# Attention in a decoder layer: the scaling of a pair of tiles and its scatter one slot further behind the scores

## What is computed

```python
x = x + attention(layernorm(x), ...)                 # 8 heads, low-rank q and kv
x = x + experts1(layernorm(x), ctx, ...)              # 8 experts of width 512, the best 2 by ctx @ Wg + bg
x = x + experts2(layernorm(x), ...)                   # 32 experts of width 64, the best 8, and a shared one

# attention, for each sequence:
scores = einsum('bhsd,bhtd->bhst', q, k) * scale
attn = softmax(scores)
o = einsum('bhst,bhtd->bhsd', attn, v_c)
return o.reshape(b, s, H * DK) @ W_O + b_O
```

## Time and profile before

| | us |
|---|---|
| median of three runs | 674.77 |
| lowest and highest of them | 673.5 and 676.57 |
| the profiled execution, its own time | 676.88 |
| the span that its trace covers | 674.8 |
| of the span: from its start to PE's first product of F1 | 197.6 |

### The profile page before, as it was taken

One profiled execution on the slowest core, in us unless ns is written; L12 is line 12 of the kernel. 1 busy time (PEld: TensorE's weight loads), 2 busy tenths in 40 slices (PEclk: granted clock), 3 DMA queues, 4 the chain that ended last, 5 costly groups with the idle time before them and its releaser, 6 DMA issues.

```text
span 674.8 us, 11558 instructions
## 1 busy us (share of the span) xinstructions
PE 620.7 (92%) x3354; PEld 464.3 (69%) x3354; DVE 543.1 (80%) x1361; ACT 421.0 (62%) x775; POOL 344.9 (51%) x410
## 2 busy tenths in 40 slices
PE   8987888887859999999889989999999999999997
PEld 7655566555647888787767656777777767677873
DVE  4687799999976666876764787899999999989973
ACT  3684678774449998888776444664737566473530
POOL 6134858888775567874674663553808255000000
PEclk9987779998889999999899999999999999999999
DMA  8998013102434555544316734544536354444551
GB/s 216 308 384 250 17 52 102 33 32 60 124 95 129 173 169 167 182 156 157 94 68 156 157 82 110 151 119 123 147 96 174 94 149 121 127 113 124 146 158 31
DMA packets 77836, 90.20 MB, mean 134 GB/s; under 512 B 15361, under 2 KB 44011, under 8 KB 77774
## 3 DMA queue, kind: packets, MB, share of 16 engines
q1 hardware_dynamic: 72648, 80.96, 42.2%
q0 software_dynamic: 4288, 8.40, 4.3%
q10 hardware_dynamic: 838, 0.11, 0.1%
HBM read 64.48 MB, written 24.90 MB: 132 GB/s over the span
## 4 chain that ended last, share of the span: by engine, by line
PE 66%; DVE 10%; issue 5%; POOL 4%; ACT 3%; DVEq 0%; ACTq 0%
PE bank L1635 10%; PE bank L1637 10%; PE bank L1636 10%; PE pair_banks L1917 7%; PE pair_banks L1537 5%; PE score_banks L1635 4%; PE score_banks L1637 4%; PE score_banks L1636 4%; POOL x_sorted L606 3%; PE pair_banks L1635 2%; PE pair_banks L1637 2%; PE pair_banks L1636 2%; PE pair_banks L1722 1%; PE bank L1537 1%; POOL sm L590 1%
## 5 line engine op out<-in xcount | busy, mean ns | idle before, releaser
L967 ACT ACTIVATE r_s<-bank 128x512 f32<-128x512 f32 x136 | 80.7, 595 | 68.0 <-PE bank L1637 66.1
L1442 DVE TENSOR_TENSOR t_s<-rc_s,bcb 128x512 f32<-128x512 f32 x128 | 89.4, 701 | 4.8 <-PE pair_banks L1917 4.8
L606 POOL DMA_INDIRECT x_sorted<-xsb,posi x64 | 63.9, 998 | 28.5 <-issue 15.1
L681 POOL DMA_INDIRECT yg<-y_sorted,posi x64 | 68.9, 1077 | 17.6 <-issue 16.9
L1429 DVE TENSOR_TENSOR rc_s<-r_s,score_banks 128x512 f32<-128x512 f32 x90 | 61.2, 680 | 18.7 <-ACT r_s L967 15.3
L1635 PE MATMUL bank<-fxh,Gh 128*128 128x512 f32 x136 | 73.3, 539 | 0.0
L733 ACT ACTIVATE t_h<-t_s 128x512 fp32r<-128x512 f32 x72 | 45.3, 629 | 41.6 <-DVE t_s L1442 27.0
L1917 PE MATMUL pair_banks<-t_s,Dn 128*128 128x512 f32 x128 | 63.2, 591 | 0.0
L1502 DVE TENSOR_TENSOR t_l<-t_s,t_h 128x512 fp32r<-128x512 f32 x72 | 53.7, 746 | 0.2
L1637 PE MATMUL bank<-fxh,Gl 128*128 128x512 f32 x136 | 53.7, 395 | 0.0
L1636 PE MATMUL bank<-fxl,Gh 128*128 128x512 f32 x136 | 53.4, 393 | 0.0
(11 more groups left out here) (327 smaller groups left out, 1822.8 us busy)
## 6 DMA issues: line engine op xcount, KB each, us to landing
bcb<-c_rows SPq DMA_DIRECT2D x128, 256.0 KB, 4.0
wraw<-in_L_xattn_W SPq DMA_DIRECT2D x46, 256.0 KB, 2.9
x_sorted<-wraw SPq DMA_DIRECT2D x1, 5888.0 KB, 18.6
y_sorted<-wraw SPq DMA_DIRECT2D x1, 5888.0 KB, 33.7
xg<-x_sorted SPq DMA_DIRECT2D x23, 256.0 KB, 2.6
y_sorted<-ysb SPq DMA_DIRECT2D x23, 256.0 KB, 2.0
ctxb<-in_ctx SPq DMA_DIRECT2D x8, 256.0 KB, 5.7
out<-x_all SPq DMA_DIRECT2D x8, 256.0 KB
```

What stands on the lines that cost most here:

```text
L606: pool.indirect_dma_start(out=xs, out_offset=bass.IndirectOffsetOnAxis(ap=posi[:, m, c:c + 1], axis=0), in_=xsb[:, m % SC, :], in_offset=N ...
L681: pool.indirect_dma_start(out=yg[:, j % 2, t, c, :], out_offset=None, in_=ys, in_offset=bass.IndirectOffsetOnAxis(ap=posi[:, j * TPS + t, ...
L967: act.activation(r_s[:, n % RB2, :], bank[n % 3][:, :], ACT.Silu).then_inc(F["act"], 1)
L1442: tt(t_s[:, n % TB2, :], rc_s[:, n % CB2, :], bcb[:, p - 1, :], ALU.mult).then_inc(F["t"], 1)
```

## The change

The scaling (`xs`) and the scatter each get a lag one higher, and the loops of all engines run one slot more.

```diff
-LAG = dict(exp=1, sum=2, norm=3, pT=4, u=5, out=6, rstd=7, xs=8, scatter=9)
+LAG = dict(exp=1, sum=2, norm=3, pT=4, u=5, out=6, rstd=7, xs=9, scatter=10)
-TAIL = 10
+TAIL = 11
```

## The result

| | before | changed |
|---|---|---|
| median, same chip, four runs each | 675.17 | 681.95 |
| lowest and highest | 673.5, 676.57 | 680.68, 682.6 |
| ratio, 95% interval | | 1.0103 [1.0081, 1.0125] |
| the profiled execution, its own time | 676.88 | 681.92 |
| its span | 674.8 | 680.1 |

The change makes the kernel 1.0% slower, about 6.8 us. The forecast was 677.2 with a range to 681.5, so it was wrong. What came looks like the rival "more eps are held, slower" (682.1), though not under the condition that the prediction gave for it.

The account below looks back on a forecast made before the run. Attention has no single busiest engine; DVE's xsb and POOL's S4 alternate on the path. Slots 9 to 14 lose about 0.7, eight pairs take 67.6 after 66.9, `xl` starts 2.4 later: 677.2 against the 674.77 median, range 671.3 to 681.5.

Parts of the forecast that it names:

- more eps are held, slower: Rival: with 0.26 or 0.5 us of DVE delay, five more pairs lose 0.98 each, +4.9 us, 682.1; chance 0.22.
- from it to S4 of slot 30, eight pairs: Slots 14 to 30 in attention: 5 x 7.97 + 3 x 8.95 + 0.9 = 67.6 us, against 66.9 before.
- What bounds the kernel, and what stays: No single busiest engine in attention; the moved step lies on the DVE-POOL path; F1 and F2 only shift.
- That N holds eps: POOL's N holds DVE's eps: 0.96 us in slots 11 and 13, and until the second N ends in bias pairs.
- the bias pair of slot 20: Pairs with bias (slots 20, 24, 28): eps asked for at 5.2, held until 6.9; pair takes 8.95 after 8.70.
- 5 x 7.97: Five pairs without bias, slots 14 to 30: 7.97 us each, as before, with eps not held.
- the low parts: Slots 25 and 27: a weight's low part follows xsb and lengthens S4's first scatter, twice 0.45, 0.9 us.
- Slots 9 to 14: DVE-bound stretch: 0.62 less xsb work, but eps held in slots 11 and 13; S4 of slot 14 at 102.3, loses about 0.7.
- So xsb is held to the end of the run, and S4 comes 0.38 later: Slots 14 to 30: xsb held through POOL's N, N, R; the pair stays 7.97 us, the 0.38 wait remains.
- POOL never waits: Rival: xsb runs at once too, pairs take 7.8 us, -5 us, 669.8; chance 0.08.
- The end: Slots 30 to F1: S4 of slot 32 at 177.8, the last R ends last at 198.7, `xl` starts at 199.3, +2.4 us.

Follow-up runs that it names:

- c_after: The changed kernel itself, word for word, run again on the second chip: 682.69 us, ratio 1.0096 to the kernel before.
- a_R_first: The changed kernel with R pulled ahead of the two N's (POOL's order S4, R, N, N): 683.71 us, ratio 1.0127 to the kernel before.
- a_no_eps: The changed kernel without eps (1e-5 not added to the variances): 678.85 us, ratio 0.994 to the kernel before; repeated 679.65 us, 0.9955.
- a_eps_single: The changed kernel with eps as two instructions of one number per partition: 680.29 us, ratio 0.9954 to the kernel before; repeats 0.9949 and 0.996.
- a_scatter11: The changed kernel with S4 one slot further behind xsb and late R's placed to match: 680.83 us, ratio 0.9969 to the kernel before.

## Why the prediction was wrong

By its own steps, against `c_after`, whose attention starts where the earlier trace rows have it:

| | forecast | `c_after` | missed |
|---|---|---|---|
| S4 of slot 14 | 102.3 | 103.84 | +1.5 |
| from it to S4 of slot 30, eight pairs | 67.6 | 70.81 | +3.2 |
| from there to `xl` | 29.4 | 29.98 | +0.6 |
| `xl` | 199.3 | 204.63 | +5.3 |

**What bounds the kernel, and what stays: right.** POOL and DVE take turns on the path, and all that follows `xl` only shifted (477.9 us in both first traces).

**That N holds eps: right.** In the slots named it came as computed, in the first trace of the changed kernel: 0.99 in slots 11 and 13 (forecast 0.96), and in the bias pair of slot 20 eps was asked for 5.36 after S4 (133.26 against 127.90, forecast 5.2) and ended 6.95 after it (forecast 6.9). The pair took 8.81, forecast 8.95. The bias itself went through in 0.69. When the hold begins, and whether R holds too, the prediction had wrong.

**The step that failed** is the pricing of the five pairs without bias, "5 x 7.97". Its times were right: eps was asked for 4.31 behind S4 with `xnl` (forecast 4.3) and 4.63 with `kvS` (forecast 4.6, 114.90 against 110.27), and N's row started at 4.86. The prediction took all that lies ahead of N's row as free, 0.26 us in the one kind and 0.5 in the other, and gave the case beyond these margins to a rival with 0.22. But there is no such margin. The N that is next in POOL's queue holds eps already during the last scatter: in four of the five pairs it was held 2.3 to 2.64 us. `a_R_first` shows that it is the queued N (0.71 us into the last scatter and free, with R next), `a_no_eps` and `a_eps_single` that nothing else made the pairs long (7.8). Where the claim begins can be narrowed with rows of two more kernels, `a_scatter11` (85 to 87) and `a_eps_single` (130 to 131), in both of which N is next:

```profile
85.46 0.96 POOL L606 DMA_INDIRECT x_sorted<-xsb,posi  x1 [0.31 <-issue]
85.67 0.17 DVE L1307 TENSOR_SCALAR mva<-mva 128x2 f32<-128x2 f32 x1
86.45 1.06 POOL L590 TENSOR_TENSOR sm<-sm,rden 128x512 f32<-128x512 f32 x1
...
130.12 0.96 POOL L606 DMA_INDIRECT x_sorted<-xsb,posi  x1 [0.30 <-issue]
130.51 2.21 DVE L1210 TENSOR_TENSOR x_all<-x_all,obb 128x512 f32<-128x512 f32 x1
131.10 1.06 POOL L590 TENSOR_TENSOR sm<-sm,rden 128x512 f32<-128x512 f32 x1
```

Asked for 0.21 us into the last scatter, eps went free; asked for 0.39 into it, the bias was held. So the claim begins between these, 0.78 to 0.59 us ahead of N's row, if it begins at the same point for both instructions, which wasn't tested; by eps alone it is 0.78 to 0.56. In slot 27 of the changed kernel eps came still earlier, 0.11 into the scatter (159.25), and was free as well.

Once eps is held, it ends with the second N, 6.94 behind S4, and S4 comes 1.86 later. So pairs take 8.80 to 8.82, with bias or without: what DVE does ahead of eps no longer counts. In `c_after` the four held plain pairs took 35.2, forecast 31.9, and this is the whole miss of the eight pairs. The rest balances. The pair from slot 26 took 8.70 without a hold of eps: 7.80, and 0.90 for two scatters that the low parts of weights lengthened (1.49 and 1.44 in the S4 at 156.70; the delay of N also left eps free). The three bias pairs took 26.9 (8.80, 8.82, and 9.25 with one more long scatter, 1.39). For these four pairs and the low parts the forecast was 35.7 (7.97, 26.85 and 0.9), and 35.6 were measured.

**Slots 9 to 14** missed by 1.5. An instruction that the sum had not looked at was held as well. These are DVE's and POOL's timelines of the changed kernel in slot 12:

```profile
95.25 1.40 DVE L1174 TENSOR_SCALAR steps<-thr,reach 128x8 f32<-128x8 f32 x1
...
94.59 0.95 POOL L606 DMA_INDIRECT x_sorted<-xsb,posi  x1 [0.30 <-issue]
95.56 1.06 POOL L590 TENSOR_TENSOR sm<-sm,rden 128x512 f32<-128x512 f32 x1
```

It took 0.23 before (96.23), and here it was asked for 0.31 ahead of N's row: the same failure, by 1.2 us; the other 0.3 wasn't traced. It belongs to the plan of blocks, eight numbers per partition, and the prediction counted only the instructions of the tile loop.

**"So xsb is held to the end of the run, and S4 comes 0.38 later": wrong, but small.** R doesn't hold xsb. In slot 27 of the changed kernel xsb is held through both N's, and ended with 0.3 of R still to run:

```profile
160.67 1.85 DVE L1234 TENSOR_SCALAR xsb<-x_all,mva 128x128 f32<-128x128 f32 x2
...
160.12 2.05 POOL L590 TENSOR_TENSOR sm<-sm,rden 128x512 f32<-128x512 f32 x2
162.12 0.72 POOL L597 TENSOR_TENSOR mva<-mva,mhalf 128x2 f32<-128x2 f32 x1
```

So a pair with free eps takes 7.8, not 7.97, with 0.20 from R's end to the scatter: the sum of the rival "POOL never waits", which the prediction gave 0.08. Had eps been free, this would have been a gain of 0.2 a pair, not none.

**The end: right in kind, 0.6 too short.** The last R was to set the last xsb, and `xl` to stand 1.3 behind R's start; it is 1.27 (203.36 to 204.63). R came 28.7 behind S4 of slot 30, forecast 28.1. The difference lies ahead of S4 of slot 32, which came 8.6 behind S4 of slot 30, forecast 7.9: DVE's own N (L1300) was held for 1 us by POOL's last N, where the prediction had allowed 0.25, for eps.

**The chances.** The rival "more eps are held" had nearly the right time, 682.1, and that is in part luck. Its condition was a delay on DVE, and there was none: eps was asked for where forecast, 4.31 and 4.63 behind S4. Its price was five pairs at 0.98, 4.9 us. Four came, at 0.84, 3.4 us, and `steps` and the end, which it didn't count, made up much of the rest. The 0.22 rested on the question whether a margin of 0.26 us holds, and the rows couldn't tell how sharp the edge of a hold is. One row of before bore on it: the bias of the earlier trace rows was asked for during R and didn't get in ahead of the N behind it. It came at 127.94, and N's row begins at 128.12. The prediction took from this only that there is no gap between two POOL instructions. The same row shows a queued N that holds ahead of its own start, by 0.18 us, and that reading would have spoken for the rival. It would not by itself have given the 0.55 us that were needed for `xnl`.

## What to carry over

When a change moves a DVE instruction near to a POOL instruction that can hold it, count what stands next in POOL's queue, not only what is running; an instruction that comes a few tenths of a microsecond ahead of the other's row isn't safe. Look at all instructions of the slot, also those that run once. Before a small instruction is moved about, look at its form: eps in two instructions of one number each costs 0.04 us more than one of two numbers, and was held in none of the six traces that have it; together with one slot more ahead of the scatter it turned a loss of 1.0% into a gain of 0.3 to 0.4%.

## What was not expected of the hardware

- The hold starts ahead of N's row, up to 0.59 us here, when a scatter runs before it: 2.63 us for eps asked for at 105.78, with N's row from 106.33, and 2.21 for the bias asked for at 130.51, with N's row from 131.10. It isn't given up between two N's. The Trainium skill (SBUF — State Buffer, Who interferes with whom) gives the pair of ports to whoever issues first; that fits, if an N issues up to that long before its row starts; what issuing is here, the traces don't show.
- POOL's R, a power of two numbers per partition, held no xsb (0.59 beside it), though it reads the same kind of memory as N. Which of its properties lets DVE's instructions pass wasn't tried.
- A copy on ACT stood up to 3.2 us, two to six times in attention, in all traces of three chips and in none of the others, and the traces name no work of this core that it waited for. The kernel before takes 7 to 9 us more on these chips, 6.0 of it in the stretch where this shows, and the ratio of the change fell from 1.010 to 1.003. The 2.4 to 4.4 us behind `xl` were not looked into.
- A place in `xsb` came free 2.95 us after the row of its last scatter in two kernels, and 3.39 in a third.
